# Moving the second head's maxima copies from VectorE to ScalarE in three units of four of the last self-attention

## What is computed

```python
ca = _mha(input_tensor, ctx_tensor, ctx_attn_mask, cq_w, cq_b, ck_w, ck_b, cv_w, cv_b)
x = _self_output(ca, input_tensor, co_w, co_b, co_g, co_be)
sa = _mha(x, x, None, sq_w, sq_b, sk_w, sk_b, sv_w, sv_b)
x = _self_output(sa, x, so_w, so_b, so_g, so_be)
inter = jax.nn.gelu(x @ fi_w + fi_b, approximate=False)
x = _self_output(inter, x, fo_w, fo_b, fo_g, fo_be)
```

## Time and profile before

| | us |
|---|---|
| median of 3 runs | 1282.24 (1278.87 to 1283.12) |
| profiled execution | 1282.84 |
| its span | 1280.4 |

### The profile page before, as it was taken

How to read it: one execution, slowest core, us unless ns; L and a number is a source line. 1 busy time by engine, 2 the same in 40 slices (tenths; PEclk the granted TensorE clock), 3 DMA queues, 4 the chain that set the end, 5 groups by cost and what they waited for, 6 DMA issues and landing times. The chain is left out here.

```text
span 1280.4 us, 33014 instructions
## 1 busy us (share of the span) xinstructions
PE 1052.6 (82%) x12028; PEld 585.6 (46%) x12028; DVE 999.3 (78%) x2503; ACT 869.9 (68%) x1778; POOL 402.5 (31%) x832
## 2 busy tenths in 40 slices
PE   4799976599999999999999999966788777188883
PEld 2455544144444444444444444433344355177772
DVE  7588856588888888888889889977799678755554
ACT  3588964188888888898898888953688743243333
POOL 3222215132150502305041141125224146555551
PEclk8699997599999999999999999998799988598997
DMA  6971007413232142313223131005720032111113
GB/s 165 217 148 39 3 2 166 118 54 91 68 93 63 37 104 82 82 53 80 68 70 96 41 76 55 8 8 121 142 36 2 2 124 74 36 34 38 37 40 113
DMA packets 76646, 92.29 MB, mean 72 GB/s; under 512 B 8463, under 2 KB 62711, under 8 KB 76488
## 3 DMA queue, kind: packets, MB, share of 16 engines
q1 hardware_dynamic: 72392, 83.90, 26.0%
q0 software_dynamic: 2496, 5.12, 1.4%
q10 hardware_dynamic: 1600, 1.18, 0.4%
HBM read 64.37 MB, written 27.02 MB: 71 GB/s over the span
## 5 line engine op out<-in xcount | busy, mean ns | idle before, releaser
L1493 DVE TENSOR_REDUCE MG<-bank 128x1 f32<-128x512 f32 x768 | 482.7, 683 | 73.2 <-PE bank L1254 71.1
L1402 ACT ACTIVATE PT<-bank 128x512 f32<-128x512 f32 (+1 forms) x624 | 335.4, 598 | 37.6 <-PE bank L1284 33.9
L1284 PE MATMUL bank<-QP,KP 54*128 54x256 bf16 (+1 forms) x1664 | 264.2, 274 | 26.0 <-ACT PT L1402 13.7
L1254 PE MATMUL bank<-KP,QP 54*128 54x512 bf16 (+1 forms) x1024 | 266.1, 342 | 14.5 <-DMA KP<-ctx_k_parts 13.8
L1304 PE MATMUL bank<-PT,VP 128*9 128x256 f32 (+1 forms) x2688 | 196.9, 366 | 0.8 <-ACT XT L1402 0.8
L1284 PEld LDWEIGHTS bank<-QP,KP 54*128 54x128 bf16 (+1 forms) x1664 | 94.1, 95 | 187.4 <-ACT PT L1402 90.3
L1582 POOL TENSOR_TENSOR MP<-MN,ZERO 128x4 bf16<-128x4 f32 x128 | 26.4, 206 | 409.1 <-DVE MN L1506 404.1
L1402 ACT ACTIVATE XT<-bank 128x512 f32<-128x512 f32 (+1 forms) x208 | 116.5, 600 | 9.9 <-PE bank L1284 8.1
L906 PE MATMUL bank<-QP,KP 51*128 51x256 bf16 x512 | 85.3, 279 | 28.3 <-DVE MN L1004 8.5
L1304 PEld LDWEIGHTS bank<-PT,VP 128*9 128x9 f32 (+1 forms) x2688 | 76.0, 90 | 55.3 <-issue 20.6
L1254 PEld LDWEIGHTS bank<-KP,QP 54*128 54x128 bf16 x1024 | 81.0, 94 | 39.5 <-issue 12.5
(11 more groups left out here) (286 smaller groups left out, 2010.2 us busy)
## 6 DMA issues: line engine op xcount, KB each, us to landing
KP<-ctx_k_parts SPq DMA_DIRECT2D x128, 100.1 KB
ctx_k_parts<-KPARTS SPq DMA_DIRECT2D x16, 600.4 KB, 5.3
KP<-ctx_k_parts SPq DMA_DIRECT2D x128, 59.4 KB
CN<-in_ctx SPq DMA_DIRECT2D x8, 768.0 KB
RAW<-in_w_gate_up SPq DMA_DIRECT2D x8, 512.0 KB, 3.7
QP<-q_parts SPq DMA_DIRECT2D x20, 192.0 KB
ctx_k_parts<-KPARTS SPq DMA_DIRECT2D x16, 200.1 KB, 5.6
UQ<-bias_table SPq DMA_DIRECT2D x4, 768.0 KB, 8.8
```

The source lines that it names most:

```text
L1254: return nc.tensor.matmul(out, k.QP[half, p, b * S + 128 * qt:b * S + 128 * (qt + 1)], k.KP[half, p, a:a + w], start=True, stop=True)
L1284: return nc.tensor.matmul(bank[0:rows[t], S * at:S * (at + 1)], k.KP[half, p, 128 * t:128 * t + rows[t]], k.QP[half, p, b * S:(b + 1) * S] ...
L1402: nc.scalar.activation(PT[n % NP][0:rows[t], :], bank_of("s", g, t)[0:rows[t], :], ACT.Exp).then_inc(exp_done, 1)
L1493: nc.vector.tensor_reduce(MG[:, g % 4, 2 * s + qt, chunk:chunk + 1], bank[:, :], AX.X, ALU.max).then_inc(m_read, 1)
```

## The change

In units with u % 4 = 1 nothing is altered: ScalarE copies the first head's rows, VectorE the second's. In the other three of four, 24 units, ScalarE copies both, the second right behind the first, and counts `m_rows` after the second; VectorE copies none. `m_rows_second` now counts once a batch, and TensorE waits for it only ahead of the scores of a unit with u % 4 = 1, and ahead of the transposes of the next unit.

```diff
                 if i == 0:
                     pe.wait_ge(m_rows, u + 1)
-                    if not bias:
-                        pe.wait_ge(m_rows_second, u + 1)
+                    if not bias and u % PER_BATCH == 1:
+                        pe.wait_ge(m_rows_second, u // PER_BATCH + 1)
...
                 if u > 0:
                     pe.wait_ge(m_rows, u)
-                    if not bias:
-                        pe.wait_ge(m_rows_second, u)
+                    if not bias and u % PER_BATCH == 2:
+                        pe.wait_ge(m_rows_second, u // PER_BATCH + 1)
...
-            heads = (0, 1) if bias else (0,)
+            def heads(u):
+                return (0,) if not bias and u % PER_BATCH == 1 else (0, 1)
+
             front.scalar(act)
             run(act_plan, {"s": exponentials, "o": read_sums,
-                           "m": lambda u, i: copy_maxima(nc.scalar.copy, act, u, heads, m_rows)})
+                           "m": lambda u, i: copy_maxima(nc.scalar.copy, act, u, heads(u), m_rows)})
...
             else:
-                actions["m"] = lambda u, i: copy_maxima(nc.vector.tensor_copy, v, u, (1,), m_rows_second)
+                def second_maxima(u, i):
+                    if u % PER_BATCH == 1:
+                        copy_maxima(nc.vector.tensor_copy, v, u, (1,), m_rows_second)
+
+                actions["m"] = second_maxima
```

## The result

The changed kernel takes 1289.12 us (median of 17 runs) against 1280.89 for the kernel before (17 runs): ratio 1.0057, 95% interval 1.0042 to 1.0071. A second comparison on the chip gave 1.0045 (1.0026 to 1.0065). It is slower, by about half a percent. The span of the profiled execution is 1288.0 us, 7.6 more.

A forecast was written before the change was run, and what follows sets the result against it. The prediction took a 3.15 us loop between ScalarE and TensorE as the bound, not VectorE. Its terms, 4.4 + 2.5 + 0.6 = 7.5 us on the 1282.24 median, gave 1289.8 us; range 1285.5 to 1293.

The forecast's parts named there:

- The bound is a loop: Last attention: ScalarE's first exponential, its copy, TensorE's scores, next exponential form a closed loop of 3.15 us, the period.
- the release: Time from the end of the last copy to TensorE's first score product: 0.25 us before, 0.14 forecast after.
- rival 4: VectorE, 94% busy, is the bound in the last attention: about 8 us faster, 1274 us; chance 0.06.
- The second copy costs 0.60: On ScalarE, a pair of copies takes 1.16 us against 0.56 for one, so the last copy ends 0.60 later.
- The dropped wait gives back 0.11: On TensorE, one wait less before the first score product shortens 0.25 us to 0.14.
- plain unit: Nine units (u % 4 = 0, and u = 3) without head sums: + 0.49 us each, 4.4 in all.
- Where it is hidden: Units with u % 4 = 2: second copy costs nothing, as TensorE does sums and values; 1.0 us of cover.
- After the head sums: Six units with u % 4 = 3, 7 to 27: first score product + 0.42 us later each, 2.5 in all.
- The tail: Unit 31, the last: its release is already 0.10, so it pays the full + 0.60 us.
- Rival 3: Beside the head sums, VectorE's earlier reductions return 3.2 us, leaving + 4.3, 1286.5 us; chance 0.11.
- Rival 2: Cheaper: ScalarE's copies run closer together than in the first attention; + 4.8, 1287.0 us; chance 0.09.
- rival 1: Dearer: the dropped wait on TensorE saves nothing, 0.25 us stays; + 9.2, 1291.4 us; chance 0.12.

The follow-up runs named there:

- shared_count: Kernel before, but both engines count one semaphore and TensorE waits once for both copies; 1275.45 us against 1279.62, ratio 0.9975.
- before_split_wait: Kernel before, but TensorE's first score product waits only for ScalarE's copy, the second for VectorE's; batch 14.57 us, last attention's stage 122.50 (before: 14.85, 124.68).
- vector_extra: Changed kernel plus one unread 128 x 512 reduction on VectorE in each of the 24 units; batch 15.75 us, last attention's stage 132.35 (changed kernel: 132.22).
- u2_only: Kernel before, but ScalarE copies both heads only in units with u % 4 = 2; batch 14.85 us, last attention's stage 124.81 (before: 124.68).
- u0_only: Kernel before, but ScalarE copies both heads only in units with u % 4 = 0; batch 15.32 us, last attention's stage 129.71 (before: 124.68).
- u3_only: Kernel before, but ScalarE copies both heads only in units with u % 4 = 3; batch 15.28 us, last attention's stage 130.41 (before: 124.68).
- copy_last: Changed kernel with ScalarE's copies behind the fourth exponential instead of ahead of it; batch 16.83 us, last attention's stage 144.14 (changed kernel: 132.22).
- after_split_wait: Changed kernel, but each head's copy is counted separately and each score product waits for its own; batch 15.56 us, last attention's stage 132.11 (changed kernel: 132.22).

## Why the prediction was right, point by point

- *The bound is a loop, not the busiest engine.* Shown for the kernel before by shared_count and before_split_wait, where taking 0.11 us out of the release takes 0.11 out of a plain unit (with the split wait 0.06 in those with u % 4 = 0) though VectorE does all its copies as before; and for the changed kernel by vector_extra, where VectorE can do 0.68 more for nothing. The rule of the Trainium skill ("Perfetto Trace Analysis", Identifying the Most-Contended Engine) that rival 4 leant on would have had this stage faster; it is slower by 7.5 us.
- *The second copy costs 0.60.* A pair takes 1.15 to 1.16. The 93 ns of overlap that the Trainium skill gives for back-to-back activations ("ScalarE: Activation LUTs", What ACT_TABLE_LOAD costs) doesn't appear between these two copies, nor between the pair and the exponential behind it, which starts 0.02 after its end (964.06 + 1.15, then 965.23). It does elsewhere: the exponential behind a single copy starts 0.46 after it, 0.10 ahead of the copy's end.
- *The dropped wait gives back 0.11.* Release 0.14 in the changed kernel and in shared_count. The size was right, the reason given (one wait less) is only part of it: which count comes last matters too, as shown above. Net 0.49 forecast for a plain unit, 0.48 and 0.47 measured.
- *Where it is hidden.* The unit beside the head sums costs nothing, by u2_only; in the changed kernel its score product starts 1.19 us after the pair's end, 1.05 more than the release needs, for 1.0 of cover forecast. After the head sums + 0.43 for + 0.42. A batch: 15.76 forecast and measured.
- *The tail.* Unit 31 was to cost 0.60 more; from its copy to the end of the division it is 10.84 for 10.21, + 0.63: 0.59 for the second copy, and 0.04 because the release there is 0.14 and no longer 0.10, which the prediction had taken as staying.
- *What follows shifts with it.* Not contradicted, and not shown finely. What follows the stage took 255.4 us before and 254.3 and 248.3 in the two profiles of the changed kernel, so single profiles can't tell whether it took some of the 7.5 us up. The medians put the change at 8.2 and 4.6 us in the two comparisons; 7.5 us (1.0059) lies in both intervals.
- *Not said in the prediction*: that ScalarE's own work, at 3.60 us a unit, stands right under the loop's 3.64. The sum didn't need it, but whoever would now repair the changed kernel by a shorter loop needs it.
- *Rival 3* fell with u2_only: the reciprocal only waits longer, 0.95 us there and 0.94 in the changed kernel for 0.36, and the gap of 5.33 stays. Rival 2 fell with the pair of 1.15, rival 1 with the release of 0.14, and rival 4 with the result and vector_extra.

## What to carry to other kernels

When several engines pass a unit round in a ring (the loop of the prediction), add the steps of the ring, releases included, and compare the sum with the period before looking at shares of busy time: an engine that is 94% busy can be paced by the ring. Work moved off it is then no gain, and work put on the ring costs its full length, unless it stands beside something longer, as one in four did here. And look at the waits that stand ahead of the instruction that closes the ring: merging two counts into one took 2.0 us off the stage, with no work moved at all. Before merging, see which of the counts comes last.

## What the runs showed of the hardware

- Waiting for two counts can cost TensorE time. From the end of the last copy to the first product it was 0.25 us with two counts, where the first one asked for came last, and 0.14 with one count, with the copies at the same distance; with two counts, and the second one asked for last, it was 0.14 to 0.15. The 0.11 us, in 17 of 32 units, made 1.9 us of stage. Why it goes by the order the runs don't show, and unit 31 (0.10 with two counts) doesn't fit.
- Two copies of 3 x 512 bf16 from PSUM follow each other on ScalarE without overlap (1.15 to 1.16 for two of 0.56 to 0.58), and the exponential behind the pair starts 0.02 after it; behind a single such copy the exponential starts 0.10 before its end.
- The granted clock may fall in the thin tail of the attention, and not in every execution. In four of twelve profiles (u0_only, u3_only, copy_last, after_split_wait) it did. In u3_only:

```profile
1015.00:1020.00 5.00, 3.45 (x53) 1.46 (x46) 2.15 (x2) 3.83 (x8) 0.59 (x3) 1.00 0.00 0
1020.00:1029.00 9.00, 7.09 (x68) 2.37 (x66) 0.00 (x0) 3.38 (x7) 0.00 (x0) 0.62 0.01 2
```

  Granted 0.62 of full speed is mostly the lower of the two levels (1.2 GHz). From unit 31's copy to the end of the division it took 13.23 us there, against 10.21 in the kernel before and 10.84 in the changed one, which has the same instructions in that part. TensorE had been 3.45 of 5 us busy just before; why it happens in one execution and not in another the runs do not settle, and no run was made on it. The tails of the four took 11.46 to 14.12 us. Against 10.21 and 10.84 that is 1.2 to 3.3 more (an estimate of the clock's part: in copy_last and after_split_wait the order or the waits differ as well), beside the 7.5 us of the change itself.
